# Layer 1 of the last four spans by rows, and idle increments ahead of TensorE's program

## The reference, cut to what matters

```python
for l in range(3):                       # GRU layers, "layer 1" is l = 0
    m = x @ weight[l]
    msg = m[src] * edge_weight[:, None]
    agg = segment_sum(msg, dst)          # 6250 x 128
    x = gru_cell(agg, x, w_ih, w_hh, b_ih, b_hh)
x = layernorm(x0 + x)
for W, b in ((W0, b0), (W1, b1), (W2, b2)):
    x = relu((x + segment_sum(x[src], dst)) @ W.T + b)
x = layernorm(x0 + x)
```

## Time and profile before

| | us |
|---|---|
| median of 3 runs | 2880.29 (2880.04 to 2880.68) |
| the profiled execution | 2883.43 |
| its span in the profile | 2881.7 |
| mean granted clock of PE | 0.993 |
| PE busy | 2832.6, 98% of the span |
| DVE, ACT, POOL busy | 1246.0, 947.4, 872.5 |

### The profile page before, as it was taken

The page is one execution under the profiler, slowest core; times in us unless marked ns, Lnnn a source line. Parts: engine busy times, 40 slices in busy tenths (PEclk is TensorE's granted clock), DMA queues, the critical chain, the costliest instruction groups (busy, mean ns, idle before and its releaser), DMA issues.

```text
span 2881.7 us, 72532 instructions
## 1 busy us (share of the span) xinstructions
PE 2832.6 (98%) x29387; PEld 1881.3 (65%) x29387; DVE 1246.0 (43%) x2716; ACT 947.4 (33%) x1891; POOL 872.5 (30%) x1007
## 2 busy tenths in 40 slices
PE   6999999999999999999999999999999999999998
PEld 5899999999999955555555555555655555555554
DVE  7678877777888514344422344343500010001011
ACT  6777777777777610000001011101400010001111
POOL 4344344443444315554541454544000000000000
PEclk7999999999999999999999999999999999999999
DMA  5666666666662398998996988988487868886884
GB/s 196 267 262 244 245 261 261 257 241 251 262 263 95 113 397 342 350 339 326 355 369 253 340 338 331 357 330 327 149 326 301 310 248 301 309 304 247 318 304 163
DMA packets 134009, 810.64 MB, mean 281 GB/s; under 512 B 17208, under 2 KB 27308, under 8 KB 113948
## 3 DMA queue, kind: packets, MB, share of 16 engines
q1 hardware_dynamic: 111228, 758.32, 67.9%
q0 software_dynamic: 19968, 40.46, 4.4%
q10 hardware_dynamic: 2720, 10.62, 0.9%
HBM read 553.01 MB, written 256.33 MB: 281 GB/s over the span
## 4 chain that ended last, share of the span: by engine, by line
PE 95%; issue 2%; DVE 1%; ACT 1%; DMA 1%; another core or an unknown queue 0%; POOL 0%; DVEq 0%; SPq 0%; ACTq 0%; POOLq 0%
PE ps L969 29%; PE ps L1165 27%; PE ps L1247 19%; PE ps L1240 11%; PE ps L979 1%; PE ps L980 1%; PE ps L1260 1%; PE ps L1261 1%; PE ps L982 1%; PE ps L981 1%; PE ps L1144 1%; ACT ring L1661 0%; DMA sum_rows<-ring 0%; PE ps L1266 0%; PE ps L1267 0%
## 5 line engine op out<-in xcount | busy, mean ns | idle before, releaser
L969 PE MATMUL ps<-ring,Y 128*128 128x448 f32 x2352 | 888.4, 539 | 0.0
L1165 PE MATMUL ps<-ring,Y 128*128 128x448 f16 x4116 | 780.6, 352 | 0.0
L1661 ACT ACTIVATE ring<-ps 128x490 f16<-128x490 f32 (+1 forms) x1344 | 698.3, 651 | 176.7 <-PE ps L1240 169.1
L969 PEld LDWEIGHTS ps<-ring,Y 128*128 128x128 f32 x2352 | 446.4, 190 | 434.8 <-issue 434.8
L1165 PEld LDWEIGHTS ps<-ring,Y 128*128 128x128 f16 x4116 | 402.7, 98 | 373.8
L863 POOL DMA_INDIRECT ring<-y_rows,ring x448 | 431.4, 963 | 518.9 <-PE ps L969 257.7
L1247 PE MATMUL ps<-ring,Y 128*128 (+1 forms) x2744 | 570.2, 360 | 0.4 <-ACT shared L1620 0.4
L1247 PEld LDWEIGHTS ps<-ring,Y 128*128 128x128 f32 x2744 | 503.6, 190 | 8.4 <-ACT shared L1620 0.8
L1240 PEld LDWEIGHTS ps<-shared 64*128 64x128 bf16 x18816 | 320.4, 93 | 76.6 <-issue 59.3
L1240 PE MATMUL ps<-shared 64*128 64x49 bf16 (+1 forms) x18816 | 346.5, 189 | 20.0 <-issue 9.6
L1824 DVE TENSOR_SCALAR ring<-ring 128x128 f32<-128x128 f32 x446 | 130.9, 294 | 388.7 <-DMA ring<-y_rows,ring 205.0
(11 more groups left out here) (196 smaller groups left out, 1450.6 us busy)
## 6 DMA issues: line engine op xcount, KB each, us to landing
ring<-adj_w SPq DMA_DIRECT2D x72, 2688.0 KB
ring<-adj_h SPq DMA_DIRECT2D x42, 2800.0 KB, 9.4
ring<-adj_h SPq DMA_DIRECT2D x42, 2688.0 KB, 9.2
adj_w<-ring SPq DMA_DIRECT2D x48, 2016.0 KB, 11.9
adj_h<-ring SPq DMA_DIRECT2D x56, 1372.0 KB, 5.4
ring<-adj_w SPq DMA_DIRECT2D x24, 2912.0 KB
adj_w<-ring SPq DMA_DIRECT2D x48, 728.0 KB, 6.8
sum_rows<-ring SPq DMA_DIRECT2D x62, 448.0 KB
```

What stands on the lines that cost most here:

```text
L969: mm = pe.matmul(ps[:, bank, 0:GW], Y[:, h, :], slab(s)[:, :, h - h0, :], start=(h == 0), stop=(last and h == TILES - 1))
L1165: mm = pe.matmul(ps[:, par, 0:GW], part[:, h, :], counts_slab(par, s)[:, :, h - h0, :], start=(h == 0 and part is Y_high), stop=(h == TILE ...
L1661: act.activation(strip[:, :, c0:c0 + UNIT * WIN].rearrange("p h (d j) -> p d h j", d=WIN)[:, :, :, w0:w1], psum_unit(a)[:, :, kind, :, :]. ...
```

## The change: what it does

- The spans are taken in the order 24, 25, 26, 27, 0 to 23 (`ORDER`). A position in this order is a slot. The first four slots are built for counts alone: no multiplication on DVE, one matmul part of 49 columns in place of three (28 matmuls a batch instead of 84), three activations a batch instead of six, two of the seven column steps, no weight strip, no `add_tiles`, no gates.
- Their layer 1 comes by rows, during slots 5 to 24: 224 rounds, 11 a slot and a twelfth in every fourth. The slot is cut into 16 half batches, and each point of the table below issues one gather on POOL, behind a wait (even: the batches before are multiplied; odd: the first unit of this batch is evacuated) and an increment of `s_mark_pool`. ACT multiplies by the weight two batches later, DVE adds four batches later, SP stores four rounds at a time. The gather goes into one of 16 buffers and is scaled and summed in place, in all layers.
- The four spans' gates come after the loop, one after another, with the last span's 49 tiles in six pieces between them (`TAIL_TILES`); the gates of span 23 come last, behind five chunks instead of three.
- The loops of DVE, ACT, POOL and SP over the spans are written out; PE's loop has 22 spans in place of 26, behind four count slots and two full ones written out.
- PE's program begins with 202 increments of a semaphore that nobody waits for (`LOOP_LEAD`).
- `run_edges` and the row buffers have their own memory and are loaded at the start, `place_ends` runs ahead of slot 25, the ends are gathered in slots 26 and 27; W1, W2 and the GRU weights move to the ring; the DMA scratch is set to 8192 bytes.
- In layers 2 and 3 the stores are of 4 rounds in place of 7, and the last two are POOL's.

```diff
-ROW_BUFS = 10
-STORE = 7
+RUN_BUFS = 16
+STORE = 4
+FIRST_RUN = GATHERS - RUN_SPANS
+ORDER = [*range(FIRST_RUN, GATHERS), *range(FIRST_RUN)]
+GATE_ORDER = [*range(FIRST_RUN - 1), *range(FIRST_RUN, GATHERS), FIRST_RUN - 1]
+RUN_SLOTS = range(RUN_SPANS + 1, GATHERS - 3)
+ROW_POINTS = [1, 2, 3, 4, 5, 7, 8, 9, 11, 12, 15]
+MORE_POINTS, MORE_EVERY = [14], 4
+SCALE_LAG, SUM_LAG, STORE_LAG = 2, 4, 5
+PLACE_SLOT, ENDS_SLOT = 25, 26
+LOOP_LEAD = 202
+TAIL_TILES = [0, 6, 15, 24, 33, 42, TILES]
...
+            def fetch_round(turn, i):
+                if i >= RUN_BUFS:
+                    if i % STORE == 0:
+                        use, q = divmod(i // STORE - STORE_TURNS, STORE_TURNS)
+                        pool.wait_ge(s_stored[q], stored_by(turn, q) + 16 * (use + 1))
+                    pool.wait_ge(s_acc, RUN * turn + i - RUN_BUFS + 2)
+                pool.indirect_dma_start(out=run_bufs[:, i % RUN_BUFS, :], out_offset=None, in_=y_rows if turn else x,
...
+            def fetch_at(t, points):
+                for point in points:
+                    i, (k, half) = round_at(t, point), divmod(point, 2)
+                    if i is None:
+                        continue
+                    if half:
+                        pool.wait_ge(s_bev, evicted(t, k) + 1)
+                    else:
+                        pool.wait_ge(s_bmm, UNITS * (BUFS + BATCHES * t + k))
+                    pool.sem_inc(s_mark_pool, 1)
...
+            def prepare_span(t):
+                fetch_at(t, range(0, 4))
...
+                add_own(t + 1, 1 - par)
+                fetch_at(t, range(4, 6))
+                take_places(t + 2, par)
...
+                for d, (k, later) in enumerate(zip(FETCH_AT, FETCH_AT[1:] + (6,))):
+                    pool.wait_ge(s_bmm, UNITS * (BUFS + n + k))
+                    pool.sem_inc(s_mark_pool, 1)
+                    gather(par, d)
+                    fetch_at(t, range(2 * k + 1, 2 * later))
+                make_columns(t + 1, 1 - par, t)
+                fetch_at(t, [14])
+                near_rows(t + 3, 1 - par)
+                fetch_at(t, [15])
...
+            for _ in range(LOOP_LEAD):
+                pe.sem_inc(s_mark_pe, 1)
...
+            for t in range(RUN_SPANS):
+                build_counts(t)
             pe.wait_ge(s_xt, NC)
-            with pe.Fori(0, GATHERS // 2 - 1) as i:
+            build_span(0, None, None, None)
+            build_span(1, 1, 0, None)
+            with pe.Fori(0, FIRST_RUN // 2 - 1) as i:
...
+            for c, n in enumerate(range(FIRST_RUN - 2, GATHERS)):
+                add_tiles(0, TAIL_TILES[c], TAIL_TILES[c + 1])
+                if n < GATHERS - 1:
+                    fused_gates(n)
...
+                if c < RUN_SPANS:
+                    flip_run(c)
```

More of the change, by code:

```diff
@@ L370, in gnn_program @@
         N_IN = 15
-        N_CONST = 16
+        N_CONST = 19
         AHEAD = 2
@@ L783, in gather, with make_columns @@
                     .then_inc(s_wsrc, 16)
-            def make_columns(t, par):
+            def make_columns(t, par, slot):
                 made = [0]
@@ new lines, in fetch_ends @@
+            def fetch_ends(turn, spans):
+                for b in range(STORES - LAST_STORES if turn else STORES, STORES):
+                    pool.wait_ge(s_acc, RUN * turn + STORE * (b + 1))
+                    pool.dma_start(sums_kept(b), sums_made(b)).then_inc(s_last, 16)
+                for q in range(STORE_TURNS):
+                    pool.wait_ge(s_stored[q], stored_by(turn + 1, q))
+                if turn:
+                    pool.wait_ge(s_last, 16 * LAST_STORES * turn)
+                if not turn:
+                    pool.wait_ge(s_place, PLACE_STEPS)
+                    pool.wait_ge(s_none, 32)
+                for span in spans:
+                    for d in range(WIN):
+                        for part in range(2):
+                            pool.indirect_dma_start(out=run_bufs[0:LANES, end_buf(span, d, part), :], out_offset=None,
+                                                    in_=sum_rows, in_offset=bass.IndirectOffsetOnAxis(
+                                                        ap=run_ends[:, part, d, span:span + 1], axis=0))\
+                                .then_inc(s_ends[span], 16)
@@ L849, in _ @@
+            for t in range(GATHERS):
+                prepare_span(t)
             pool.wait_ge(s_steps, WIN * (GATHERS + 2))
@@ L896, in _ @@
                     fetch_rows(layer)
-                    fetch_ends(layer)
+                    fetch_ends(1 + layer, range(RUN_SPANS))
             with pool.Else():
@@ L1251, in add_tiles, with flip_run, state_of @@
                         mm.then_inc(s_fagg, 1)
+            def flip_run(r):
+                n = GATE_ORDER.index(FIRST_RUN + r)
+                pe.wait_ge(s_joined, r + 1)
+                pe.wait_ge(s_fev, START + n)
+                for d in range(WIN):
+                    at = d * LANES
+                    mm = pe.matmul(ps[:, RUN_BANK, at:at + LANES], run_bufs[0:LANES, end_buf(r, d, 0), :],
+                                   ident[0:LANES, 0:LANES], start=True, stop=True)
+                mm.then_inc(s_fagg, 1)
+            def state_of(n):
+                span = GATE_ORDER[n] if isinstance(n, int) else n
+                return xT[:, bass.ds(span * SPAN, SPAN)]
             def fused_rz(n, bank):
-                xg = xT[:, bass.ds(n * SPAN, SPAN)]
+                xg = state_of(n)
                 pe.wait_ge(s_fev, START + n + 1)
@@ L1808, in rounds_by, with sum_row, sum_batch @@
                 return max(0, min(RUN, SLOT_FIRST + SLOT_NEXT * slot))
+            def sum_row(turn, i):
+                done = RUN * turn + i
+                row, last = (run_bufs[:, j % RUN_BUFS, :] for j in (i, i - 1))
+                dve.wait_ge(s_acc, done)
+                dve.wait_ge(s_prod, done - turn)
+                dve.scalar_tensor_tensor(out=row, in0=last, scalar=run_edges[:, i, 2:3], in1=row,
+                                         op0=ALU.mult, op1=ALU.add).then_inc(s_acc, 1)
+            def sum_batch(n):
+                for i in rounds_at(n):
+                    if i:
+                        sum_row(0, i)
             def add_rows(layer, slot, part=range(SLOT_NEXT)):
```

525 lines of the change are left out of this document (280 added, 245 removed).

## The result

| | median | range | runs |
|---|---|---|---|
| before | 2880.39 us | 2880.04 to 2885.78 | 5 |
| after | 2967.95 us | 2960.01 to 2969.82 | 5 |

The ratio is 1.029, its 95% interval 1.0278 to 1.0302: slower by 3%, where 1.3% faster was forecast and 2880 us was the upper end of the range. The profiled execution has a span of 2961.1 us; by the forecast it would have been 2881.7 - 35.9 = 2845.8, so 115.3 us have to be found.

What follows compares the result with a forecast made beforehand. PE's work was taken to bound the kernel, DVE and ACT close behind; stage terms summed to 951.3 against 987.2 us, 35.9 less, giving 2844 us by the median; range 2812 to 2880 us.

Steps and rivals of the forecast that it cites:

- increments, start of the build: Head of PE's program: 202 increments take 9.3 to 10.3 us, hidden by PE's 4.19 us wait for DVE; cost 0.
- four count slots: First four slots, built for counts alone: 18.75 us each, near a floor of 16, 75 us together.
- the 19 periods: PE's span loop with row gathers, from transposes to transposes: 34.2 us a span plus 1.0 a slot for gathers.
- tail: After the loop: the same passes and five sets of gates, PE's work just covering each set's chain; 32.3 us.
- layers 2 and 3, the rest: Changes to POOL, DVE and stores there run beside PE; taken as 0, bounds 2 and 5 us.
- the term for the row slots: Slots 5 to 24: row gathers delay the handover of the columns by 1.0 us a slot, 20 us in 20 slots.
- Rival 3: PE's loop: its program is fetched again in each of 21 passes, 107 us, total 2951; chance 0.04.
- The ends: Slots 26 and 27: 16 gathers in POOL's free time, DVE's small steps ahead of slot 25; 2 us, bounds 0 and 4.
- Rival 2: POOL's queue in slots 5 to 24 becomes the bound: 6.7 us a slot, 134 us, total 2958; chance 0.14.
- DVE's sums: Row slots: DVE adds a row in 0.352 us, 3.9 us a slot, 31 of 34.2, beside PE.
- ACT's scaling: Row slots: ACT scales a row in under 0.35 us, 3.9 us a slot, 30.4 of 34.2, beside PE.
- the prediction's second sum: POOL in row slots: gathers slowed to 1.287 us by the shared DVE port; 2.4 us a slot, 28 us longer.

Runs made afterwards that it cites:

- f2: Changed kernel with its 202 increments moved from the head to behind the four count slots; 2946.51 us.
- h3: g2 with its 160 increments spread, 40 behind each of the four count slots and none at the head; 2888.27 us.
- h1: Changed kernel with 160 increments at the head and 42 more in PE's branch that never runs; 2898.74 us.
- g1: Changed kernel with 96 increments at the head in place of 202; 3085.24 us.
- g2: Changed kernel with 160 increments at the head in place of 202; 2899.27 us.
- e2: Changed kernel without the 208 row gathers of layer 1 that reuse a buffer, a semaphore raised in their place; 2852.34 us.
- i1: h4 with each row scaled, summed and stored one batch later (lags 3, 5, 6 in place of 2, 4, 5); 2841.47 us.
- h4: h3 with the row gathers of points 12 to 15 issued behind the column copies and the near gather; 2891.07 us.
- f1: Changed kernel run once more, nothing edited, on chip 6; 2957.96 us.
- e1: Changed kernel with no increments at the head of PE's program (LOOP_LEAD = 0); 2964.85 us.

## Why the prediction was wrong

Own time of the profiled execution, against the terms of the sum:

| step | forecast | measured | miss |
|---|---|---|---|
| increments, start of the build | 0 | 18.5 (45.49 for 26.97) | +18.5 |
| four count slots | 75 | 77.3 | +2.3 |
| slot 4 to the first transposes of a row slot (29 + 0.6 x 34.5) | 49.7 | 51.9 | +2.2 |
| the 19 periods (0.4 x 34.5 + 42.3 + 17.6 x 35.2) | 675.6 | 744.7 | +69.1 |
| to the end of slot 27, with the ends | 118.7 | 139.6 | +20.9 |
| tail | 32.3 | 32.7 | +0.4 |
| layers 2 and 3, the rest | 0 | 1.9 | +1.9 |

The misses add up to the 115.3 us. In two places the prediction failed. Its largest miss is the term for the row slots: it added 1.0 us a slot, for the handover of the columns alone, and 5.0 were measured. And it took the increments as 46 to 51 ns each and covered; they are 155 ns each, and 18.5 us of them came through.

**The increments were mis-sized, at both ends.** I priced one at 46 to 51 ns from a register operation. Start of the first matmul with 0, 96, 160, 202 and 234: 8.63, 19.83, 29.60, 36.17, 41.14. From 96 on that is 0.155 us each, three times the price, so 202 are some 31 us, against a cover of 4.19 us and what PE waits for ahead of the build; 18.5 us came through. f2 got back 11.5 us by moving them behind the count slots, h3 10.5 (against h1, on the same chip): the cover is there, not at the head.

**Rival 3 did not come true, and the increments are why.** With 0 and 96 of them the loop's code was fetched again, 128 and 254 packets. A period of g1 is 45.7 us, 8.5 more than g2's, where the prediction priced a refetch at 5.1 us. With 160, 202 and 234 the code stayed. The Trainium skill ("Runtime: NRT & Kernel Launch", section "Instruction fetch mechanics") gives PE room for 2048 instructions in blocks of 256. The traces agree in so far as a body of that size stayed for some starts and not for others. But the nine packets a pass in g1 are more than the seven or eight blocks that the prediction worked out.

**The row slots failed in a way that no rival had.** The prediction said 1.0 us a slot, by the columns. Without row gathers (e2) the 19 periods take 657.1 us, 87.6 less than in the changed kernel, and 50.1 less than in g2, which has all gathers and ran on e2's chip. In the changed kernel what PE waits for is the pauses inside bursts: 46.7 us for "issue", 1.2 for DVE. The sum had no term for them. They hide a second loss. Where the pauses are gone (g2, chip 15) the 19 periods are 37.5 us shorter (9.8 us less idle time, 27.7 us less that counts as busy, 665.50 against 693.15, for the same matmuls), and they are still 31.6 us over the forecast, with PE waiting 40.6 us for DVE. So the two losses overlap, and the runs do not say what either costs by itself. The waits of DVE were of my kind, POOL late and DVE late by it, but I worked out one handover out of three: the columns. The near gather queues behind row gathers too (by the group rows above, 42.0 us in 15 slots), and ACT has to wait for a row's landing. i1 takes 48.0 us from g2 (707.2 - 659.2) by order and lag, and comes out at 34.7 us a period, under my 35.2. No run has the order and lag of i1 together with the pauses.

**The ends.** The stretch after the 19 periods took 20.9 us more than forecast; its two periods with the ends' gathers took 46.4 and 45.0 us. In every kernel without pauses and without refetches there (g1 has nine packets in each) they took 34.2 us each. Their price as POOL's work was right.

**Rival 2 came near in time (2958) and was wrong in kind.** POOL is busy for 453 of 744.7 us, and with every gather in place i1's PE is busy for 652 of 659. Its price of 1.97 us a gather fell: behind a satisfied wait a gather mostly starts after 0.16 to 0.31 us.

**Right:** count slots, tail, layers 2 and 3, and DVE's sums (0.35 us a row). ACT's scaling took 0.429 us a row, where under 0.35 was taken; ACT is busy for 566.65 of the 744.7 us, so it had the room.

**A gather's length follows DVE.** Row gathers took 1.198 us in the mean over the build, and 0.961 in layers 2 and 3. The timeline of the changed kernel shows what the longer ones have in common:

```profile
600.57 1.24 DVE L2290 TENSOR_TENSOR shared<-shared 128x2100 bf16<-128x2100 bf16 x1
600.78 1.85 POOL L894 DMA_INDIRECT run_bufs<-in_x,run_edges  x1 [0.30 <-issue]
```

From 150 to 1000 us 152 gathers start with over 0.2 us of one of DVE's three large one-hot operations (L2284, L2286, L2290) still to run; they end 0.82 us behind it in the median and take 1.45 us in the mean. The 135 that start with none of the three running take 0.97. This agrees with the port rule that I weighed (the Trainium skill, "SBUF — State Buffer", section "SBUF: two separate sides"), with the gather as the one that waits: DVE's product of 2100 columns takes 1.247 us from 280 to 870 us, against 1.272 in the earlier trace rows. It makes POOL later, as the 1.287 us of the prediction's second sum would; how much of the miss that is, no run tells.

The forecast of 2844 us is near what i1 reached (2841.47), a program with another order, other lags and other increments. That it is so near is partly luck: i1's four count slots take 85.4 us for the 75 forecast, its 19 periods 659.2 for 675.6.

## What to carry to other kernels

Price an instruction that "does nothing" on the engine it is put on, and put it where that engine is seen to wait; where padding is used to place a loop, try several lengths and look at the instruction queue's packets. When a difference between two programs rests on something that the profile doesn't name, run both on the same chip: the kernel before was run beside every experiment here, the changed one beside one group only, and so its pauses have two explanations left. When work is put into a queue, follow every item that is queued behind it to its consumer, not only the first: here three waits had to be moved before any of the time came back, and removing one alone (h4) gained nothing. And give transfers whose consumer is an in-order engine a lag that covers their landing.

## What the runs showed of the hardware

- A semaphore increment at the head of PE's program costs about 0.155 us (first matmul at 19.83, 29.60, 36.17 and 41.14 us with 96, 160, 202 and 234 of them).
- PE's issue can be held for 0.5 to 1.2 us at a time while GpSimd works on an indirect gather, with no instruction packet and no semaphore in sight, in steps of about 0.7 us with one to six small matmuls between them. In the changed kernel 53 of 152 bursts were cut, in g2 one. A second build showed the same on chip 6 (f1, 91 pauses). Whether it goes by the programs' lengths or by the chip is open.
- Behind one such burst the granted clock fell to 0.52 (the lower level), and the 14 additions took 5.49 us where 2.92 is usual, so a pause can cost more than its length.
- A gather of GpSimd that starts while one of DVE's large one-hot operations runs ends about 0.82 us behind it (median of 152 in the changed kernel; 25 such gathers in the kernel before: 0.81 us).
- e1's loop, fetched anew in some passes, varies by 31 us from run to run; g1's, fetched anew in each, by 4.9; those that stay by 0.2 to 9.8.
